# Adapters with transposes three units behind, y's two parts taken straight from PSUM, and a shared normalisation

## Chip, cores and metric

One core of one Trainium2 chip. The metric is the device time of one execution in microseconds. The kernel before: median 1236.32 us of three runs (1235.46, 1236.32, 1237.9).

## The reference

`x` is (4, 512, 512) in float32: 4 sequences of 512 positions, 512 features. Layer 0 is attention, two GELU networks with a hidden size of 2048 and a clip to 0..1 (its result is called y0 here). The change leaves it alone. Then come three adapters, L1 to L3, of the same form, with weights picked by sequence out of three experts:

```python
h = jnp.einsum('bsh,bhk->bsk', hidden_states, W_down[role]) + b_down[role][:, None, :]
h = jax.nn.gelu(h, approximate=False)          # (4, 512, 256)
u = jnp.einsum('bsk,bkh->bsh', h, W_up[role]) + b_up[role][:, None, :]
y = hidden_states + u
mean = jnp.mean(y, axis=-1, keepdims=True)
var = jnp.mean(jnp.square(y - mean), axis=-1, keepdims=True)
yn = (y - mean) * jax.lax.rsqrt(var + LN_EPS)
return yn * gamma[role][:, None, :] + beta[role][:, None, :]
```

## The kernel before

The kernel is written with hand-made queues: a fixed order of instructions for each engine, semaphores between them. Layer 0 fills the first 1057 us. The adapters follow as twelve **units**: unit u is layer u // 4 of sequence u % 4. So unit u needs the result of unit u - 4. All products are made in three passes of fp32r: an operand is kept as a high part and a low part, and `mm3` (L538) multiplies high by high, high by low, low by high.

A unit goes through these stages:

- down products D(u), `t_down_mm` (L692): 24 matmuls 128x512 from yT[u % 4] (features on partitions, high and low part) into two PSUM banks (`down_bank`)
- `h_gelu` (L1019) on ACT: GELU with the down bias into hf, then a cast to the high part in h_hl; `h_lo` (L1405) on DVE: the low part
- up products U(u), `t_up_mm` (L713): 24 matmuls into banks 0 to 3 (`UP`), positions on partitions
- `z_stats` (L1416) on DVE: four tiles, each the sum of PSUM and the residual rows `res` into z, then bn_stats and bn_aggr
- GpSimd (POOL, L1509): ve and rstd of a unit, two small instructions; `factors` (L1399) on DVE: nmr = -mean x rstd
- `z_norm` (L1013) on ACT: z = z x rstd + nmr, four tiles in place
- POOL (L1525, L1527): the residual rows of unit u + 4, res = z x gamma + (beta + next up bias), eight instructions of 128x512 a unit (units 0 to 7)
- transposes T(u), `t_transpose` (L727): 16 transposes of z into four PSUM banks (`tr_bank`, L198)
- `y_scale` (L1033) on ACT: yf = T x gamma + beta for four tiles out of PSUM, then four casts to yT's high part; `y_lo` (L1450) on DVE: low part = yf - high part. For units 8 to 11 the scaled tiles are the output instead

The order of the work is that of four loops over steps s. PE (L753): D(s), U(s-1), T(s-2). ACT (L1048): z_norm(s-2), h_gelu(s), y_scale(s-2). DVE (L1465): h_lo(s), z_stats(s-1) with the factors of s-1 at its end, y_lo(s-2). POOL: for each unit rstd, then all its residual rows. In steps 0 to 2, y0 of sequences 1 to 3 is transposed to rows on PE (`y0_to_rows`, L674) and the first up bias added by DVE (`y0_rows`, L1389). z has two buffers, at u % 2. For the last two units (`FINE`, L339) rstd and factors are made in halves; the last unit's z tiles 1 and 3 are normalised by DVE (`norm_tile`, L1410) and its output tiles 1 and 3 scaled by DVE (`out_scale`).

SP issues all loads and stores in order. `unit_columns` (L480) loads gamma, beta and down bias of a unit as columns into one of four places (`pp`), from unit 4 on after y_scale(u-4). Around it stand the loads of weights (`unit_down`, `unit_up`) and of the rows for POOL (`unit_rows`). Line L509 loads y0 of sequence 1.

Of the kernel before, what the change touches and what calls it, by code (L numbers as in the profile page):

```python
# [12 lines left out]
P = 128  # L13
B = 4
# [84 lines left out]
def build(nc, wts, xin, bias_in, codes_in, experts_in, up_w, dn_w, wdu_all, pp_all, gb_all,  # L99
          bup_all, out):  # L100
    ctx = ExitStack()
    with ctx:
# [48 lines left out]
        z = [at("z0", 104, [P, DT, V]), at("z1", 136, [P, DT, V])]  # L151
# [19 lines left out]
        pp = sm[:, 84:124].rearrange("p (b n) -> p b n", b=B)  # L171
# [99 lines left out]
        t_pp = [sem(f"unit_columns_landed_{i}") for i in range(B)]  # L271
# [67 lines left out]
        FINE = 10  # L339
# [23 lines left out]
        def _(sp):  # L363
# [116 lines left out]
            def unit_columns(u, layer, b):  # L480
                if u >= B:
                    sp.wait_ge(t_yf, (u - 4) * DT + DT)
                row = layer * EXPERTS + ex[b]
                sp.dma_start(pp[:, b, :], pp_all[bass.ds(row, 1)].rearrange("o p n -> (o p) n")).then_inc(t_pp[b], 16)
# [18 lines left out]
            for b in range(B):  # L503
                sp.dma_start(bup0[:, b, :], bup_all[bass.ds(ex[b], 1)].to_broadcast([P, V])).then_inc(t_bup0, 16)
                unit_columns(b, 0, b)
            sp.wait_ge(aop_used, PAIRS * AOP)
            unit_up(0)
# [7 lines left out]
            for u in range(2, 14):  # L515
                if u < 12:
                    unit_down(u)
                    if u >= B:
                        unit_columns(u, u // B, u % B)
# [17 lines left out]
        def _(pe):  # L537
# [154 lines left out]
            def t_down_mm(u, b):  # L692
                pe.wait_ge(t_wd[u % 2], 16 * (u // 2 + 1))
                for m in range(MT):
# [3 lines left out]
                    elif u == 2:  # L698
                        pe.wait_ge(t_hf, (u - 2) * MT + m + 1)
                    else:  # L700
                        pe.wait_ge(t_yf, (u - 3) * DT + m + 1)
# [25 lines left out]
            def t_transpose(u, b):  # L727
                for d in range(DT):
                    if u == 11:
                        pe.wait_ge(t_z, 12 * DT)  # L730
                    elif u == 10 and d >= 2:
                        pe.wait_ge(t_yf, (u - 1) * DT + d - 1)
                    elif d >= 2:
                        pe.wait_ge(t_hf, (u + 2) * MT + d - 1)
                    elif u:
                        pe.wait_ge(t_yf, (u - 1) * DT + d + 3)
                    else:
                        pe.wait_ge(t_hf, MT + d + 1)
                    for i in range(DT):
                        if d == 0 and u == 11:  # L740

                            if i % 2:
                                pe.wait_ge(t_znv, i // 2 + 1)
                            else:
                                pe.wait_ge(t_zn, 11 * DT + i // 2 + 1)
                        elif d == 0:
                            pe.wait_ge(t_zn, u * DT + (i + 1))
                        ins = nc.tensor.transpose(tr_bank(u, d)[:, i * P:(i + 1) * P],
                                                  z[b % 2][:, i, d * P:(d + 1) * P], ident[:, :])
# [3 lines left out]
            for s in range(14):  # L753
                if s < 12:
                    t_down_mm(s, s % B)
                if s == 0:
                    y0_to_rows(1)
                if 1 <= s < 13:
# [3 lines left out]
                if 2 <= s:  # L762
                    t_transpose(s - 2, (s - 2) % B)
# [3 lines left out]
        def _(act):  # L767
# [245 lines left out]
            def z_norm(u, tiles=range(DT)):  # L1013
                for i in tiles:
                    act.wait_ge(t_nmr, nmr_count(u, i))
                    nc.scalar.activation(z[u % 2][:, i, :], z[u % 2][:, i, :], ACT.Identity,  # L1016
                                         scale=rstd[:, u % 2, i:i + 1], bias=nmr[:, u % 2, i:i + 1]).then_inc(t_zn, 1)

            def h_gelu(u):  # L1019
                for m in range(MT):  # L1020
                    act.wait_ge(t_down, u * MT + m + 1)
                    if m == 0:
                        act.wait_ge(t_pp[u % B], 16 * (u // B + 1))
                    if u > 0:
                        act.wait_ge(t_hlo, (u - 1) * MT + m + 1)
                    nc.scalar.activation(hf[m][:, :], down_bank(u, m), ACT.Gelu, bias=pp[:, u % B, 8 + m:9 + m]).then_inc(t_hf, 1)
# [5 lines left out]

            def y_scale(u, tiles=range(DT)):  # L1033

                for d in tiles:
                    act.wait_ge(t_tr, u * DT + d + 1)
                    if 1 <= u < 8:
                        act.wait_ge(t_ylo, (u - 1) * DT + d + 1)
                    dst = yf[d][:, :] if u < 8 else res[:, u % B, d, :]
                    nc.scalar.activation(dst, tr_bank(u, d), ACT.Identity,  # L1040
                                         scale=pp[:, u % B, d:d + 1], bias=pp[:, u % B, 4 + d:5 + d]).then_inc(t_yf, 1)
                if u < 8:
                    for d in range(DT):
                        act.wait_ge(t_yf, u * DT + d + 1)
                        nc.scalar.copy(yT[u % B][:, 0, d, :], yf[d][:, :]).then_inc(t_yhi, 1)
# [20 lines left out]
        def _(dve):  # L1066
# [343 lines left out]
            def norm_tile(i):  # L1410

                dve.wait_ge(t_nmr, nmr_count(11, i))
                nc.vector.tensor_scalar(z[1][:, i, :], z[1][:, i, :], rstd[:, 1, i:i + 1], nmr[:, 1, i:i + 1],
                                        ALU.mult, ALU.add).then_inc(t_znv, 1)

            def z_stats(u):  # L1416

                for i in range(DT + 2):
                    if i < DT:
# [3 lines left out]
                        if u >= 2:  # L1423

                            if u < 10:
                                dve.wait_ge(t_rmul, (u - 2) * DT + i + 1)
                            dve.wait_ge(t_tr, (u - 1) * DT)
# [156 lines left out]
```

## Time and profile before

| | |
|---|---|
| median of three runs | 1236.32 us |
| the profiled execution | 1239.01 us |
| its span, first to last instruction | 1236.9 us |
| PE (matmuls) busy | 1191.9 us, 96% |
| DVE busy | 807.4 us, 65% |
| ACT busy | 567.0 us, 46% |
| POOL busy | 173.5 us, 14% |
| granted TensorE clock, mean | 0.994 |
| adapters | about 1057 us to the end |

The page's second part shows the span in 40 equal slices of 31 us. Each digit is the busy share in tenths, 9 is 90% or more. The adapters are the last six slices:

```profile
PE   7999999799999899999999999989999999999997
DVE  5444385746766766565766666686665565879986
POOL 1332230000000000000000000000000000488871
PEclk9999999899999999999999999999999999999999
```

PE is TensorE's matmuls, DVE VectorE, ACT ScalarE, POOL GpSimd, SP the engine that issues the loads (its queue is SPq). L12 is line 12 of the kernel. A "releaser" is the instruction whose semaphore ended an idle time. Records of neighbouring instructions on ACT and DVE overlap by some 0.1 us, so the step from one start to the next is shorter than a record.

### The profile page before, as it was taken

The page shows a single profiled execution, that of the slowest core. Times are in us where ns is not written, and L with a number is a line of the kernel's source. Part 1 is how long each engine was busy: PE and PEld are TensorE (multiplying, and loading weights), DVE is VectorE, ACT ScalarE, POOL GpSimd, SP SyncE. Part 2 cuts the span into 40 slices and gives each one's busy share as a digit, 9 for nine tenths or more (in the row PEclk, how much of TensorE's full clock was granted, in tenths as well). Part 3 has the DMA queues.
Part 4 walks back from the last instruction along what each step waited for, and adds up shares of the span by engine and source line. Part 5 has one row for each costly group of instructions (what it writes and reads, how often), then busy time and mean ns, then how long its engine had stood idle before and what let it go on. Part 6 is the DMA issues. An engine that isn't in the chain of part 4 may idle for free.

```text
span 1236.9 us, 15228 instructions
## 1 busy us (share of the span) xinstructions
PE 1191.9 (96%) x5312; PEld 973.7 (79%) x5312; DVE 807.4 (65%) x1461; ACT 567.0 (46%) x1068; POOL 173.5 (14%) x147
## 2 busy tenths in 40 slices
PE   7999999799999899999999999989999999999997
PEld 5878878677788688888887787768888888788776
DVE  5444385746766766565766666686665565879986
ACT  5334353554533534343524633544343433266666
POOL 1332230000000000000000000000000000488871
PEclk9999999899999999999999999999999999999999
DMA  5755452114312202020461221411111118655534
GB/s 189 271 199 180 162 176 85 43 43 153 122 58 77 87 16 94 10 94 9 169 274 51 88 83 51 171 51 51 52 52 52 52 34 322 229 189 193 175 137 170
DMA packets 51186, 145.82 MB, mean 118 GB/s; under 512 B 6420, under 2 KB 6420, under 8 KB 46886
## 3 DMA queue, kind: packets, MB, share of 16 engines
q1 hardware_dynamic: 51110, 144.84, 33.2%
q8 instruction: 43, 0.70, 0.2%
q14 instruction: 33, 0.27, 0.1%
HBM read 108.11 MB, written 36.71 MB: 117 GB/s over the span
## 4 chain that ended last, share of the span: by engine, by line
PE 71%; DVE 11%; POOL 8%; ACT 4%; issue 4%; DMA 1%; SPq 0%; POOLq 0%; DVEq 0%; ACTq 0%
PE psum L541 70%; POOL res L1525 3%; POOL res L1527 3%; DVE ring L1187 1%; DMA prep<-wdu_dram 1%; ACT z L1016 1%; ACT ring L877 1%; POOL sm L1518 1%; DVE g_hl L1254 1%; DVE sm L1434 1%; DVE res L1269 1%; DVE res L1324 1%; DVE w_t L1228 0%; DMA wk_raw<-wts_dram 0%; POOL prep L1498 0%
## 5 line engine op out<-in xcount | busy, mean ns | idle before, releaser
L541 PE MATMUL psum<-g_hl,w_hl 128*128 128x512 f32 x1536 | 353.3, 390 | 1.5 <-DVE g L1242 1.3
L541 PE MATMUL psum<-a_op,ring 128*128 128x512 f32 x1344 | 324.4, 394 | 17.5 <-DVE w_t L1228 11.1
L541 PEld LDWEIGHTS psum<-g_hl,w_hl 128*128 128x128 f32 x1536 | 287.9, 188 | 64.6 <-DVE g L1242 4.8
L541 PEld LDWEIGHTS psum<-a_op,ring 128*128 128x128 f32 x1344 | 252.9, 190 | 77.8 <-DVE w_t L1228 14.5
L541 PE MATMUL psum<-c_op,ring 128*128 128x512 f32 x672 | 166.1, 394 | 0.6 <-DVE c_op L1296 0.6
L1254 DVE TENSOR_TENSOR g_hl<-g,g_hl 128x512 fp32r<-128x512 f32 x128 | 87.7, 691 | 111.7 <-ACT g_hl L917 110.4
L541 PEld LDWEIGHTS psum<-c_op,ring 128*128 128x128 f32 x672 | 127.3, 190 | 28.5 <-DVE c_op L1296 2.0
L1506 POOL TENSOR_TENSOR yT<-res,yT 128x512 fp32r<-128x512 f32 x8 | 11.7, 1487 | 875.6 <-ACT yT L1011 875.6
L877 ACT CAST ring<-asum 128x256 fp32r<-128x256 f32 x192 | 76.2, 403 | 122.3 <-PE psum L541 100.9
L917 ACT CAST g_hl<-g 128x512 fp32r<-128x512 f32 x128 | 78.3, 618 | 101.1 <-PE psum L541 101.1
L1187 DVE TENSOR_TENSOR ring<-asum,ring 128x256 fp32r<-128x256 f32 x192 | 80.8, 422 | 63.8 <-ACT ring L877 61.3
L894 ACT ACTIVATE g<-g,sm 128x512 f32<-128x512 f32 x96 | 69.6, 725 | 109.9 <-DVE g L1234 47.5
L1187 DVE TENSOR_TENSOR ring<-rawp,ring 128x256 fp32r<-128x256 f32 x144 | 60.8, 422 | 81.0 <-ACT ring L877 81.0
L1269 DVE TENSOR_TENSOR res<-psum,res 128x512 f32<-128x512 f32 x96 | 64.8, 691 | 24.1 <-PE psum L541 24.0
L877 ACT CAST ring<-rawp 128x256 fp32r<-128x256 f32 x144 | 57.0, 403 | 46.3 <-PE psum L541 46.2
L541 PE MATMUL psum<-yT,wd 128*128 128x512 f32 x288 | 68.6, 394 | 6.0 <-issue 6.0
L1498 POOL TENSOR_TENSOR prep<-prep 128x512 f32<-128x512 f32 x36 | 51.6, 1437 | 131.4 <-ACT prep L788 131.4
L541 PE MATMUL psum<-wu,h_hl 128*128 128x512 f32 x288 | 67.4, 390 | 0.0
L541 PEld LDWEIGHTS psum<-yT,wd 128*128 128x128 f32 x288 | 53.1, 188 | 18.0 <-issue 7.3
L541 PEld LDWEIGHTS psum<-wu,h_hl 128*128 128x128 f32 x288 | 54.0, 188 | 11.2
L1016 ACT ACTIVATE z<-z,sm 128x512 f32<-128x512 f32 x46 | 33.9, 808 | 37.7 <-DVE sm L1402 37.7
L1525 POOL TENSOR_TENSOR res<-z,bc 128x512 f32<-128x512 f32 x32 | 48.2, 1507 | 12.4 <-ACT z L1016 12.4
(124 smaller groups left out, 1381.2 us busy)
## 6 DMA issues: line engine op xcount, KB each, us to landing
rawp<-up_w_dram SPq DMA_DIRECT2D x48, 512.0 KB, 3.6
wdu_split<-prep SPq DMA_DIRECT2D x36, 512.0 KB, 2.9
wraw<-dn_w_dram SPq DMA_DIRECT2D x64, 256.0 KB, 3.1
wd<-wdu_split SPq DMA_DIRECT2D x12, 1024.0 KB, 7.3
wu<-wdu_split SPq DMA_DIRECT2D x12, 1024.0 KB, 5.4
prep<-wdu_dram SPq DMA_DIRECT2D x36, 256.0 KB, 3.3
second_pair_operands<-c_op SPq DMA_DIRECT2D x7, 1024.0 KB, 6.9
a_op<-second_pair_operands SPq DMA_DIRECT2D x7, 1024.0 KB, 11.3
```

What stands on the lines that cost most here:

```text
L541: ins = nc.tensor.matmul(ps, lw(el), rw(er), start=first and i == 0, stop=last and i == 2, skip_group_check=skip)
L877: nc.scalar.copy(ring[n % RING][:, 0, :], aop_src(n)).then_inc(aop_hi, 1)
L894: nc.scalar.activation(dst, src, ACT.Gelu, bias=(cb1, mb1)[l][:, t:t + 1]).then_inc(gelu_done, 1)
L917: nc.scalar.copy(g_hl[t % GHL][:, 0, :], g[:, q, 2 * row + seq, :]).then_inc(g_hi_done, 1)
L1016: nc.scalar.activation(z[u % 2][:, i, :], z[u % 2][:, i, :], ACT.Identity, scale=rstd[:, u % 2, i:i + 1], bias=nmr[:, u % 2, i:i + 1]).the ...
L1187: nc.vector.tensor_tensor(ring[n % RING][:, 1, :], aop_src(n), f(ring[n % RING][:, 0, :]), ALU.subtract).then_inc(aop_lo, 1)
L1254: nc.vector.tensor_tensor(g_hl[t % GHL][:, 1, :], g[:, q, 2 * row + seq, :], f(g_hl[t % GHL][:, 0, :]), ALU.subtract).then_inc(g_lo_done, 1)
L1269: nc.vector.tensor_tensor(dst, bank[4 * seq + m], dst, ALU.add).then_inc(d_evac, 1)
L1324: nc.vector.tensor_scalar(res[:, 2 + seq, m, :], res[:, 2 + seq, m, :], 0.0, 1.0, ALU.max, ALU.min).then_inc(y0_done, 1)
L1498: nc.gpsimd.tensor_tensor(prep[i][:, 1, :], prep[i][:, 1, :], prep[i][:, 0, :], ALU.subtract).then_inc(p_lo, 1)
L1525: nc.gpsimd.tensor_tensor(res[:, u % B, i, :], z[i2][:, i, :], bc[i2][:, 0, :], ALU.mult).then_inc(t_rmul, 1)
L1527: nc.gpsimd.tensor_tensor(res[:, u % B, i, :], res[:, u % B, i, :], bc[i2][:, 1, :], ALU.add).then_inc(t_res, 1)
```

## The change

Seven things are changed, all in the adapters.

1. PE transposes a unit one step later: D(s), T(s-3), U(s-1). The banks of the transposes change: tiles 0 and 1 go to UP[2] and UP[3], tiles 2 and 3 to the down banks of the same parity. The up products of tiles 2 and 3 wait until tiles 0 and 1 of y (unit u - 2) have been read out by DVE.
2. z has three buffers (u % 3).
3. `y_split` and `y_less_high` take the place of y_scale's first part, the casts and y_lo for units 0 to 7. ACT makes yT's high part straight from PSUM (T x gamma + beta, rounded). DVE makes yf = T x gamma - high part from PSUM with one scalar_tensor_tensor a tile, and ACT adds beta to it, which is the low part.
4. Every unit's z tiles 0 and 2 are normalised by ACT, 1 and 3 by DVE (`norm_tile`), ahead of y_less_high in DVE's order.
5. ACT's step: GELU(s), y_split(s-3), h_hi(s), z_norm(s-2). DVE's step: factors(s-2), two norm_tiles, y_less_high(s-3), z_stats(s-1), h_lo(s).
6. POOL's order for a unit: rstd(u), residual rows 2 and 3 of u - 1, residual rows 0 and 1 of u.
7. All twelve units' columns are loaded at once, at a place of their own, after the last use of layer 0's operands. Only the last unit is made in halves (`FINE` 11).

```diff
-        z = [at("z0", 104, [P, DT, V]), at("z1", 136, [P, DT, V])]
+        z = [at(f"z{i}", k, [P, DT, V]) for i, k in enumerate((104, 136, 128))]
...
-            return bank[4 + 2 * ((u % 2) ^ (1 if d < 2 else 0)) + d % 2]
+            if u == 10:
+                return bank[4 + d]
+            return UP[2 + d] if d < 2 else bank[4 + 2 * (u % 2) + d - 2]
...
+            for u in range(LAYERS * B):
+                unit_columns(u)
...
+                    if u >= 2 and i >= 2:
+                        pe.wait_ge(t_yf, (u - 2) * DT + i - 1)
...
-            for s in range(14):
+            for s in range(15):
                 if s < 12:
                     t_down_mm(s, s % B)
                 if s == 0:
                     y0_to_rows(1)
+                if 3 <= s:
+                    t_transpose(s - 3, (s - 3) % B)
                 if 1 <= s < 13:
                     t_up_mm(s - 1, (s - 1) % B)
                 if 1 <= s < 3:
                     y0_to_rows(s + 1)
-                if 2 <= s:
-                    t_transpose(s - 2, (s - 2) % B)
...
-            def z_norm(u, tiles=range(DT)):
-                for i in tiles:
+            def z_norm(u):
+                for i in (0, 2):
                     act.wait_ge(t_nmr, nmr_count(u, i))
-                    nc.scalar.activation(z[u % 2][:, i, :], z[u % 2][:, i, :], ACT.Identity,
+                    nc.scalar.activation(z[u % 3][:, i, :], z[u % 3][:, i, :], ACT.Identity,
                                          scale=rstd[:, u % 2, i:i + 1], bias=nmr[:, u % 2, i:i + 1]).then_inc(t_zn, 1)
...
+            def y_split(u):
+
+                for d in range(DT):
+                    act.wait_ge(t_tr, u * DT + d + 1)
+                    nc.scalar.activation(yT[u % B][:, 0, d, :], tr_bank(u, d), ACT.Identity,
+                                         scale=pp[:, u, d:d + 1], bias=pp[:, u, 4 + d:5 + d]).then_inc(t_yhi, 1)
+                for d in range(DT):
+                    act.wait_ge(t_yf, u * DT + d + 1)
+                    nc.scalar.activation(yT[u % B][:, 1, d, :], yf[d][:, :], ACT.Identity,
+                                         bias=pp[:, u, 4 + d:5 + d]).then_inc(t_ylo, 1)
...
-            for s in range(12):
-                if 2 <= s < 11:
-                    z_norm(s - 2)
-                h_gelu(s)
-                if s == 11:
-                    z_norm(9)
+            for s in range(14):
+                if s < 12:
+                    h_gelu(s)
+                if 3 <= s < 11:
+                    y_split(s - 3)
+                if 11 <= s:
+                    y_scale(s - 3)
+                if s < 12:
+                    h_hi(s)
                 if s == 0:
                     y0_hi(3)
                 if 2 <= s:
-                    y_scale(s - 2)
-            z_norm(10)
-            y_scale(10)
-            z_norm(11, (0, 2))
+                    z_norm(s - 2)
             y_scale(11, LAST_BY[0])
...
+            def norm_tile(u, i):
+
+                dve.wait_ge(t_nmr, nmr_count(u, i))
+                nc.vector.tensor_scalar(z[u % 3][:, i, :], z[u % 3][:, i, :], rstd[:, u % 2, i:i + 1], nmr[:, u % 2, i:i + 1],
                                         ALU.mult, ALU.add).then_inc(t_znv, 1)
...
+            def y_less_high(u):
                 for d in range(DT):
                     dve.wait_ge(t_yhi, u * DT + d + 1)
-                    nc.vector.tensor_tensor(yT[u % B][:, 1, d, :], yf[d][:, :], f(yT[u % B][:, 0, d, :]), ALU.subtract).then_inc(t_ylo, 1)
+                    if u >= 1:
+                        dve.wait_ge(t_ylo, (u - 1) * DT + d + 1)
+                    nc.vector.scalar_tensor_tensor(out=yf[d][:, :], in0=tr_bank(u, d), scalar=pp[:, u, d:d + 1], in1=f(yT[u % B][:, 0, d, :]),
+                                                   op0=ALU.mult, op1=ALU.subtract).then_inc(t_yf, 1)
...
             for s in range(13):
-                if s < 12:
-                    h_lo(s)
+                if 2 <= s:
+                    factors(s - 2, 0, DT)
+                    norm_tile(s - 2, 1)
+                    norm_tile(s - 2, 3)
+                if 3 <= s < 11:
+                    y_less_high(s - 3)
                 if s == 0:
                     y0_rows(1)
                 if 1 <= s < 13:
                     z_stats(s - 1)
                 if 1 <= s < 3:
                     y0_rows(s + 1)
-                if 2 <= s < 10:
-                    y_lo(s - 2)
-            norm_tile(3)
+                if s < 12:
+                    h_lo(s)
             out_scale(11)
...
+            def next_rows(u, tiles):
+
+                pool.wait_ge(t_bc[u % 2], 32 * (u // 2 + 1))
+                for i in tiles:
+                    pool.wait_ge((t_zn, t_znv)[i % 2], 2 * u + i // 2 + 1)
+                    nc.gpsimd.tensor_tensor(res[:, u % B, i, :], z[u % 3][:, i, :], bc[u % 2][:, 0, :], ALU.mult).then_inc(t_rmul, 1)
                     pool.wait_ge(t_rmul, u * DT + i + 1)
-                    nc.gpsimd.tensor_tensor(res[:, u % B, i, :], res[:, u % B, i, :], bc[i2][:, 1, :], ALU.add).then_inc(t_res, 1)
+                    nc.gpsimd.tensor_tensor(res[:, u % B, i, :], res[:, u % B, i, :], bc[u % 2][:, 1, :], ALU.add).then_inc(t_res, 1)
+
+            for u in range(12):
+                rstd_of(u)
+                if 1 <= u < 9:
+                    next_rows(u - 1, (2, 3))
+                if u < 8:
+                    next_rows(u, (0, 1))
```

The rest of the diff renames the buffers and their semaphore counts to fit: rstd of u waits for z_norm and norm_tile of u - 2 each, z's writing waits for T(u-3) and for POOL's reading of u - 3, and D(u) for u >= 4 waits until y_less_high(u-4) has read the down banks.

## Rows read from the trace of the kernel before

**Rows 1.** Window view, one unit: us, busy PE, PEld, DVE, ACT, POOL, clock, DMA share, GB/s

```profile
1142.80:1157.50 14.70, 13.24 (x66) 10.66 (x65) 13.18 (x20) 9.86 (x17) 13.02 (x10) 1.00 0.52 179
```

**Rows 2.** Chain of waits, one unit: start us, us, what

```profile
1142.78 0.82 ACT z L1016
1143.74 1.37 POOL res L1525
...
1154.58 1.29 POOL res L1527
1156.22 1.03 POOL sm L1518
1157.47 0.82 ACT z L1016
```

**Rows 3.** Timeline of PE where nothing holds it: start us, us, instructions

```profile
1067.06 5.72 PE L541 MATMUL psum<-yT,wd 128*128 128x512 f32 x24
1072.62 5.61 PE L541 MATMUL psum<-wu,h_hl 128*128 128x512 f32 x24
1078.06 1.91 PE L688 MATMUL psum<-ident,res 128*128 128x128 f32 x16
...
1079.72 5.70 PE L541 MATMUL psum<-yT,wd 128*128 128x512 f32 x24
...
1090.71 1.69 PE L688 MATMUL psum<-ident,res 128*128 128x128 f32 x12
```

**Rows 4.** Timeline of the other engines in one unit, same columns

```profile
1142.66 4.67 DVE L1453 TENSOR_TENSOR yT<-yf,yT 128x512 fp32r<-128x512 f32 x4
...
1146.76 1.13 ACT L1031 CAST h_hl<-hf 128x512 fp32r<-128x512 f32 x2
...
1147.40 3.31 DVE L1408 TENSOR_TENSOR h_hl<-hf,h_hl 128x512 fp32r<-128x512 f32 x2
...
1150.63 1.27 DVE L1428 TENSOR_TENSOR z<-psum,res 128x512 f32<-128x512 f32 x2
...
1155.54 0.29 DVE L1440 BATCH_NORM_AGGREGATE sm<-sm 128x2 f32<-128x6 f32 x2
```

**Rows 5.** Source view of one DVE line, and its timeline beside GpSimd's subtractions

```profile
L1324 DVE TENSOR_SCALAR res<-res x8: 417/962/1529, 1057.0 to 1062.7; 128x512 f32<-128x512 f32 x8
...
1059.83 1.51 DVE L1324 TENSOR_SCALAR res<-res 128x512 f32<-128x512 f32 x1
1061.27 1.51 DVE L1324 TENSOR_SCALAR res<-res 128x512 f32<-128x512 f32 x1
```

**Rows 6.** Source views of lines: duration ns min/median/max

```profile
L1413 DVE TENSOR_SCALAR z<-z,sm x2: 545/546/546, 1228.5 to 1230.1; 128x512 f32<-128x512 f32 x2
...
L1428 DVE TENSOR_TENSOR z<-psum,res x48: 650/674/692, 1075.3 to 1225.9; 128x512 f32<-128x512 f32 x48
...
L1266 DVE SCALAR_TENSOR_TENSOR res<-psum,sm,res x16: 750/751/751, 455.9 to 876.9; 128x512 f32<-128x512 f32 x16
...
L894 ACT ACTIVATE g<-g,sm x96: 722/725/728, 228.5 to 1035.4; 128x512 f32<-128x512 f32 x96
```

**Rows 7.** Timeline of VectorE at factors(1) and factors(8)

```profile
1095.84 0.16 DVE L1402 SCALAR_TENSOR_TENSOR sm<-sm 128x4 f32<-128x4 f32 x1 [1.42 <-POOL sm L1518]
...
1201.37 0.16 DVE L1402 SCALAR_TENSOR_TENSOR sm<-sm 128x4 f32<-128x4 f32 x1 [1.45 <-POOL sm L1518]
```

**Rows 8.** Timelines of the tail: VectorE, then PE

```profile
1218.72 0.66 DVE L1428 TENSOR_TENSOR z<-psum,res 128x512 f32<-128x512 f32 x1
...
1220.56 0.16 DVE L1440 BATCH_NORM_AGGREGATE sm<-sm 128x2 f32<-128x6 f32 x1
...
1220.12 5.71 PE L541 MATMUL psum<-wu,h_hl 128*128 128x512 f32 x24
```

**Rows 9.** Timeline of the load queue, and the landing of one load

```profile
1048.74 0.34 SPq L509 DMA_DIRECT2D res<-y_spill  x1
...
DMA to landing us min/median/max: 10.8/10.8/10.8
```

More of the change, by code:

```diff
@@ L270, in build @@
         t_wu = [sem(f"up_weights_landed_{i}") for i in range(2)]
-        t_pp = [sem(f"unit_columns_landed_{i}") for i in range(B)]
+        t_pp = sem("unit_columns_landed")
         t_bc = [sem(f"unit_rows_landed_{i}") for i in range(2)]
@@ L337, in y_ready @@
             return (t_yf, u * DT + by_act.index(d) + 1) if d in by_act else (t_yv, by_dve.index(d) + 1)
-        FINE = 10
+        FINE = 11
         LAST_BY = (0, 2), (1, 3)
@@ L478, in unit_up, with unit_columns @@
                              split_sets[bass.ds(u // B * EXPERTS + ex[b], 1), DT * KB // PC:NPC].rearrange("o c p e n -> p e (o c) n")).then_inc(t_wu[u % 2], 16)
[L480 to L484, printed above, removed]
+            def unit_columns(u):
+                row = u // B * EXPERTS + ex[u % B]
+                sp.dma_start(pp[:, u, :], pp_all[bass.ds(row, 1)].rearrange("o p n -> (o p) n")).then_inc(t_pp, 16)
             def unit_rows(u, layer, b):
@@ L730, in t_transpose @@
                         pe.wait_ge(t_z, 12 * DT)
-                    elif u == 10 and d >= 2:
-                        pe.wait_ge(t_yf, (u - 1) * DT + d - 1)
+                    elif u == 10:
+                        pe.wait_ge(t_yf, (u - 2 + d // 2) * DT + d % 2 + 3)
                     elif d >= 2:
@@ L1021, in h_gelu, with h_hi @@
                     act.wait_ge(t_down, u * MT + m + 1)
-                    if m == 0:
-                        act.wait_ge(t_pp[u % B], 16 * (u // B + 1))
+                    if u == 0 and m == 0:
+                        act.wait_ge(t_pp, 16 * LAYERS * B)
                     if u > 0:
                         act.wait_ge(t_hlo, (u - 1) * MT + m + 1)
-                    nc.scalar.activation(hf[m][:, :], down_bank(u, m), ACT.Gelu, bias=pp[:, u % B, 8 + m:9 + m]).then_inc(t_hf, 1)
+                    nc.scalar.activation(hf[m][:, :], down_bank(u, m), ACT.Gelu, bias=pp[:, u, 8 + m:9 + m]).then_inc(t_hf, 1)
+            def h_hi(u):
                 for m in range(MT):
@@ L1036, in y_scale @@
                     act.wait_ge(t_tr, u * DT + d + 1)
[L1037 to L1045, printed above, removed]
-            y0_hi(2)
-            for s in range(12):
-                if 2 <= s < 11:
-                    z_norm(s - 2)
-                h_gelu(s)
-                if s == 11:
-                    z_norm(9)
+                    nc.scalar.activation(res[:, u % B, d, :], tr_bank(u, d), ACT.Identity,
+                                         scale=pp[:, u, d:d + 1], bias=pp[:, u, 4 + d:5 + d]).then_inc(t_yf, 1)
+            y0_hi(2)
+            for s in range(14):
[7 more added lines that the diff above has]
+                    h_hi(s)
                 if s == 0:
@@ L1422, in z_stats @@
                             dve.wait_ge(t_res, (u - B) * DT + i + 1)
[L1423 to L1427, printed above, removed]
-                        nc.vector.tensor_tensor(z[u % 2][:, i, :], UP[i], res[:, u % B, i, :], ALU.add).then_inc(t_z, 1)
+                        if u >= 3:
+                            if u < 11:
+                                dve.wait_ge(t_rmul, (u - 3) * DT + i + 1)
+                            dve.wait_ge(t_tr, (u - 2) * DT)
+                        nc.vector.tensor_tensor(z[u % 3][:, i, :], UP[i], res[:, u % B, i, :], ALU.add).then_inc(t_z, 1)
                     if 1 <= i < DT + 1:
@@ L1442, in z_stats @@
                         factors(u, 0, 2)
-                if u == 11:
-                    norm_tile(1)
                 if u >= FINE:
+                    norm_tile(u, 1)
                     factors(u, 2, 2)
-                else:
-                    factors(u, 0, DT)
-            def y_lo(u):
+                    norm_tile(u, 3)
+            def y_less_high(u):
                 for d in range(DT):
                     dve.wait_ge(t_yhi, u * DT + d + 1)
-                    nc.vector.tensor_tensor(yT[u % B][:, 1, d, :], yf[d][:, :], f(yT[u % B][:, 0, d, :]), ALU.subtract).then_inc(t_ylo, 1)
+                    if u >= 1:
+                        dve.wait_ge(t_ylo, (u - 1) * DT + d + 1)
+                    nc.vector.scalar_tensor_tensor(out=yf[d][:, :], in0=tr_bank(u, d), scalar=pp[:, u, d:d + 1], in1=f(yT[u % B][:, 0, d, :]),
+                                                   op0=ALU.mult, op1=ALU.subtract).then_inc(t_yf, 1)
             def out_scale(u):
@@ L1458, in out_scale @@
                     dve.wait_ge(t_tr, u * DT + d + 1)
-                    nc.vector.tensor_scalar(res[:, u % B, d, :], tr_bank(u, d), pp[:, u % B, d:d + 1], pp[:, u % B, 4 + d:5 + d],
+                    nc.vector.tensor_scalar(res[:, u % B, d, :], tr_bank(u, d), pp[:, u, d:d + 1], pp[:, u, 4 + d:5 + d],
                                             ALU.mult, ALU.add).then_inc(t_yv, 1)
@@ L1508, in _, with rstd_of @@
             pool.wait_ge(s_half, 1)
-            for u in range(12):
+            def rstd_of(u):
                 i2 = u % 2
```

38 lines of the change are left out of this document (11 added, 27 removed).

## Prediction

> **What bounds the kernel now.** Read the table of 40 slices on the page first: PE is busy at 9 tenths in nearly every slice at a granted clock of 0.9 or more, so the first 1057 us are TensorE's matter and the change leaves them as they are. What is left is the adapters, the last 180 us. There the table of windows [rows 1] shows something else: a unit takes 14.70 us, PE is busy 13.24 us of it, DVE 13.18 and POOL 13.02, so no busy share decides. The chain of waits does [rows 2]: it never goes through PE, but round a loop of ACT, POOL and DVE. ACT normalises tile 0 of a unit (1142.78), POOL starts the next layer's residual rows 0.96 us later, works eight row operations until 1155.87 and then the two small ones for rstd until 1157.25; DVE makes the shifts, ACT normalises the next unit at 1157.47. One turn is 14.69 us, and the turns from the third unit to the ninth are alike. POOL idles in it only while it waits for ACT. PE without a hold [rows 3] needs 5.55 us for the down products (1067.06 to 1072.62), 5.44 for the up products (to 1078.06) and 1.66 for sixteen transposes (to 1079.72): 12.65 us. So 2.0 us a unit are to be won by a better order and no more, about 15 us over seven units.
>
> In what follows F(u) is the moment at which DVE starts factors(u), the shifts of unit u. In the trace F(1) is 1095.84 and F(8) is 1201.37 [rows 7]; from F(8) to the end of the span are 35.5 us.
>
> **The change, part by part.** The third z buffer and POOL's new order (rstd of u, rows 2 and 3 of u-1, rows 0 and 1 of u) are meant to let POOL work through. They take the wait for ACT off rows 2 and 3, but rows 0 and 1 of u still stand ahead of rstd of u+1, and they wait for tile 0 of unit u, which ACT normalises at the very end of its step. I follow that loop, since every instruction of it is in program order:
>
> F(u), DVE: factors, 0.16 us [rows 7] and 0.04 until the next starts: 0.20.
>
> DVE: norm_tile(u,1) and norm_tile(u,3). Alone such an instruction takes 0.55 us (L1413) [rows 6]. But POOL starts rows 2 and 3 of u-1 as soon as rstd is made, about 0.1 us ahead of the first norm_tile. What a scale-and-shift from SBUF to SBUF costs DVE beside a POOL tensor_tensor is in [rows 5]: 417 ns alone, but 1.51 us each, one every 1.44 us, while POOL subtracts: each waits out one whole POOL operation. The first norm_tile then ends 1.55 us after its issue and the second 1.44 later: 3.0. Bounds: 1.1 (both free, 2 x 0.55), 2.0 (one free, one held), 3.0 (both held). I take 3.0, as four such instructions in a row were held (two of them stand in the rows).
>
> By the Trainium skill, "SBUF — State Buffer", section "Who interferes with whom", a tensor_scalar can run in a mode that takes the port pair shared with GpSimd, and whoever starts second is blocked for the whole instruction. The 1.51 us of [rows 5] agree. By that rule alone, whoever issues first decides, so it would give 1.1 if DVE came first; that is the rival below.
>
> DVE: y_less_high(u-1, 0), a scalar_tensor_tensor with one input in PSUM: 0.75 (L1266) [rows 6]. Held or not? The z addition has the same kinds of places, PSUM and SBUF in, SBUF out, and was at most 0.69 us in 48 (L1428) [rows 6] although POOL was busy beside most of them. I take it as free; its upper bound is that of the old y_lo, which has both inputs in SBUF: 4.67 us for four [rows 4].
>
> ACT: hand-over 0.05, then y_split's second half. Its four activations follow DVE's 0.67 us steps (0.75 less the overlap of records): three steps, 2.0, and the last with 0.05 and 0.57 until the next starts, since a bias-only activation from SBUF has a record of 0.725 (L894) [rows 6]: 2.62. Bounds 2.6 and 2.9 (the 0.82 of z_norm, which also scales).
>
> ACT: h_hi, two casts in 1.02 (the record of 1.13 [rows 4] less the overlap). ACT: z_norm(u,0) and hand-over to POOL: 0.96 [rows 2].
>
> POOL: rows 0 and 1, four operations. Eight took 12.13 us [rows 2], 1.52 each with DVE's contending operations beside them; DVE's h_lo will again lie in this stretch (3.31 us for two where POOL is active, [rows 4]). Four at 1.52: 6.08; bounds 5.2 (four of 1.29 alone) and 6.9 (four at up to 1.72).
>
> POOL: rstd of u+1, 1155.87 to 1157.25: 1.38, and 0.03 to DVE. Then F(u+1).
>
> Sum: 0.20 + 3.0 + 0.75 + 0.05 + 2.62 + 1.02 + 0.96 + 6.08 + 1.38 + 0.03 = 16.1 us a unit, against 14.69. In general it is 13.1 + N, with N the time of the two norm_tiles.
>
> Does anything else close later? DVE's own step is 0.2 + 3.0 + 2.75 + 5.2 for z_stats (1150.63 to 1155.83, [rows 4]) + 3.3 for h_lo = 14.5: it idles 1.6 us for the factors. POOL's is 12.1 + 1.4 = 13.5. PE: the up products now wait at tile 2 for y_less_high of the transposes in the same banks, that is F + 3.95; half of the up products, down products, transposes and the other half are 12.65 us, so PE idles some 3.4 us a unit, ahead of tile 2 above all. The y parts come in time for the down products (first at F + 4.7, wanted at F + 6.7). Making the y parts directly from PSUM removes 2.19 us of copies from ACT's hi path and DVE's 4.67 us become 2.75; both lie on engines that then wait, apart from what the sum above holds.
>
> **Ahead of the loop.** D(3) no longer has T(0) before it, and U(1) ends at 1090.7 as before [rows 3]. DVE then has the last addition and statistics (2.0, as 1218.72 to 1220.72 in [rows 8], from 1090.9), the fourth residual (four at 0.62, as the z addition's record of 0.69 less overlap) and now h_lo(2) ahead of factors(1), beside POOL's rows: 2 x 1.6. F(1) is 1090.9 + 2.0 + 2.5 + 3.2 = 1098.6, 2.8 later than before. Column loads: twelve instead of four are issued before the weights and y0 of sequence 1. Eight more at some 0.5 us of queue are 4 us; y0 of sequence 1 was issued at 1048.74 and landed in 10.8 [rows 9], at 1059.5, and PE transposes it directly ahead of D(1), which starts at 1067.06 [rows 3]; the sixteen transposes take 1.7 us and end there, so some 5 us hide it. I put it at nothing; 0 to 2 us if the queue is slowed twice as much. The later loads lose their column load and the wait ahead of it, which were no bound.
>
> **The tail.** From F(8): up products of unit 9 go on at F + 3.95 and end at 6.7, D(11) at 12.25, T(8) at 13.9, U(10) at 19.35; DVE ends the statistics of unit 10 at 21.4 (0.2 and 2.0 behind), and only then h_lo(11), 0.6 each: U(11) can begin at 22.1. Before, it began at 1220.12 and the span ended 16.8 us after that [rows 8]; what follows U(11) is unchanged. So 38.9 us instead of 35.5: +3.4 (36 + N in general).
>
> **The sum.** 1098.6 + 7 x 16.1 + 38.9 = 1250.2 us of span, against 1236.9: +2.8 ahead of the loop, +7.2 in seven turns (112.7 against 105.5), +3.4 in the tail, 13.4 in all. The profiled execution took 1239.01 us, 2.1 more than its span and 2.7 more than the median of the runs; I add the difference to the median: 1236.32 + 13.4 = 1249.7.
>
> **The rivals.** (1) The norm_tiles find the port free (N = 1.1). DVE's chain from rstd to the first norm_tile is 0.23 us and POOL's next start some 0.1, so it is a race that the profile of before does not show. If DVE wins it and keeps the port for both, F(1) is 1097, the turn 14.2, the tail 37.1: 1233.5 of span, 1232.9 us. This is the case on the other side; in terms of N the span is 1223.8 + 8.8 N, so it decides below N = 1.5. (2) One held, one free: N = 2.0, 1241.4 of span, 1240.8 us. (3) The loop does not bind, because ACT's tile is early by something I overlook, and PE's 12.65 us do: 1097 + 88.6 + 37.1 = 1222.7, 1222.1 us. For it: the busy sums of ACT and DVE fall. Against it: each step of the loop is held by program order or by a semaphore. (4) y_less_high is held by POOL too, two of four, some 1.1 more each: eight turns (tail included) of 2.2 more, 1267 us. Against it: the record of L1428 [rows 6].
>
> **Chances.** Forecast, 1245 to 1254: 0.47. Rival 2, up to 1244: 0.16. Rival 4: 0.04. Rival 1: 0.14, a mixture of 1 and 2 within 0.2% of before: 0.09. Rival 3: 0.10. A difference of 0.2% (2.5 us) is about what a measurement of this kernel tells from none. So faster 0.24, same 0.09, slower 0.67. The range of eight in ten leaves out rival 3 and rival 4: 1231 to 1255, where the lower bound of POOL's rows (0.9 a turn) is only reached together with rival 1's N.
>
> **What would show it.** A turn of the chain near 16 us that goes through DVE norm, y_less_high, ACT y_split, h_hi, z_norm, POOL rows and rstd; norm_tile records of 1.5 to 1.6 us for units 1 to 8 and 0.55 for 9 to 11; y_less_high at 0.75; PE idle before L541, released by DVE's y_less_high, about 3 us a unit; DVE waiting for POOL's rstd. Wrong would be: norm_tiles at 0.55 throughout, a chain that stays on PE, POOL without idle time, or an h_lo that is late for the up products.

## The result: slower by 1.6%, the loop was right, one of its terms was not

Median of four runs 1258.94 us (1254.94 to 1260.75) against 1237.11 us for the kernel before (four runs, one more than the 1236.32 us above rest on). The ratio is 1.0164, 95% interval 1.0142 to 1.0186. I had forecast 1249.7 with 1231 to 1255: the right sign, 13.4 us where 21.8 were measured, and the time lies above the range. The profiled execution took 1258.94 us, its span 1257.2 (before 1236.9).

The busy sums are no guide: in the changed kernel ACT is busy 8.7 us less (558.3 us) and POOL 4.2 us less (169.3), and DVE 16.4 us more (823.8). The windows view of one unit of the changed kernel, columns as in [rows 1]:

```profile
1146.55:1163.62 17.07, 14.60 (x66) 11.84 (x65) 14.48 (x22) 9.25 (x15) 12.43 (x11) 0.90 0.45 156
```

A unit takes 17.07 us (before 14.70), no engine is full, and the granted clock is 0.90 instead of 1.00. The chain of waits over the same unit, start us, us, what, in place of the chain in [rows 2]:

```profile
1146.55 1.27 DVE sm L1401
1148.60 0.64 issue
1149.37 1.48 DVE z L1412
1150.85 0.67 DVE yf L1451
1151.54 2.00 ACT yT L1038 x3
1153.62 0.53 issue
1154.15 1.12 ACT h_hl L1028 x2
1155.27 0.73 ACT z L1011
1156.13 1.31 POOL res L1527
1157.51 1.30 POOL res L1529
1158.81 1.70 POOL res L1527
1160.59 1.61 POOL res L1529
1162.29 0.19 POOL sm L1518
1162.57 1.03 POOL sm L1520
1163.62 1.26 DVE sm L1401
```

L1401 are the factors, L1412 norm_tile, L1451 y_less_high, L1038 the second half of y_split, L1028 h_hi, L1011 z_norm, L1527 and L1529 residual rows, L1520 rstd. It is the loop that the prediction summed, link by link. One turn is 17.07 us here and 17.04 on the mean of the six from the second on. The first link is the surprise: 1.27 us for an instruction on four numbers a partition, 0.16 in [rows 7]. Who stands beside it is in the timelines of DVE and POOL:

```profile
1146.55 1.26 DVE L1401 SCALAR_TENSOR_TENSOR sm<-sm 128x4 f32<-128x4 f32 x1 [2.56 <-POOL sm L1520]
1147.84 3.00 DVE L1412 TENSOR_SCALAR z<-z,sm 128x512 f32<-128x512 f32 x2
1150.77 2.71 DVE L1451 SCALAR_TENSOR_TENSOR yf<-psum,unit_columns,yT 128x512 f32<-128x512 f32 x4
...
1146.49 1.30 POOL L1527 TENSOR_TENSOR res<-z,bc 128x512 f32<-128x512 f32 x1
1147.87 1.29 POOL L1529 TENSOR_TENSOR res<-res,bc 128x512 f32<-128x512 f32 x1
1149.12 1.44 POOL L1527 TENSOR_TENSOR res<-z,bc 128x512 f32<-128x512 f32 x1
```

POOL's row begins at 1146.49, DVE's factors at 1146.55, and they end together, at 1147.8. Then each norm_tile waits out one more POOL operation and ends 0.3 us behind it. By the records the first norm_tile starts 0.03 us before that operation (1147.84 against 1147.87) and is still the one that waits, so starts this close do not show who came first. y_less_high is not held: four in 2.71 us, the first two of them beside a POOL operation (1150.64 to 1151.97). PE in the same unit:

```profile
1146.18 3.01 PE L540 MATMUL psum<-wu,h_hl 128*128 128x512 f32 x12
1151.65 4.57 PE L540 MATMUL psum<-wu,h_hl 128*128 128x512 f32 x12 [2.47 <-DVE yf L1451]
1156.06 5.64 PE L540 MATMUL psum<-yT,wd 128*128 128x512 f32 x24
```

It does tiles 0 and 1 of the up products, idles 2.47 us for y_less_high (forecast 3.4), and then takes 4.4 us for tiles 2 and 3 instead of 2.7. The windows view tells why; the clock is the column behind POOL's:

```profile
1149.20:1151.65 2.45, 0.00 (x0) 0.03 (x1) 2.45 (x4) 0.11 (x1) 2.37 (x2) 1.00 0.00 0
1151.65:1156.06 4.41, 4.41 (x12) 3.50 (x13) 4.41 (x8) 4.41 (x8) 0.32 (x1) 0.61 0.37 123
1156.06:1161.54 5.48, 5.48 (x25) 4.46 (x24) 5.00 (x10) 1.32 (x2) 5.25 (x4) 1.00 0.67 219
```

After the idle stretch the granted clock is 0.61 on the mean, mostly the 1.2 GHz level, and 1.00 again for the down products. The prediction had no term for this. It gives a second account of the same 17.07 us: PE's own 12.65, 2.5 of waiting and 1.7 of low clock also make 16.9. The experiments had to tell the two apart.

### The profile page after: what moved, and what is told of

Its sections match the earlier page's. It is cut to its first block, busy times and chain, and to the rows that moved or that the text cites. A ratio compares the mean times of both kernels' runs of the same rounds, so it can differ in the third digit from the quotient of the medians.

```text
span 1257.2 us, 15252 instructions
## 1 busy us (share of the span) xinstructions
PE 1201.5 (96%) x5312; PEld 981.5 (78%) x5312; DVE 823.8 (66%) x1482; ACT 558.3 (44%) x1046; POOL 169.3 (13%) x145
## 4 chain that ended last, share of the span: by engine, by line
PE 71%; DVE 12%; ACT 5%; POOL 5%; issue 4%; DMA 2%; SPq 0%; DVEq 0%; POOLq 0%; ACTq 0%
PE psum L540 70%; DMA prep<-wdu_dram 2%; POOL res L1527 2%; POOL res L1529 2%; DVE ring L1186 1%; ACT yT L1038 1%; DVE z L1412 1%; ACT ring L872 1%; DVE sm L1401 1%; DVE g_hl L1253 1%; POOL sm L1520 1%; ACT h_hl L1028 1%; POOL prep L1500 1%; DVE res L1323 1%; DVE res L1268 1%
## 5 line engine op out<-in xcount | busy, mean ns | idle before, releaser
L540 PEld LDWEIGHTS psum<-a_op,ring 128*128 128x128 f32 x1344 | 252.7, 189 | 77.7 <-DVE w_t L1227 14.6
L540 PE MATMUL psum<-wu,h_hl 128*128 128x512 f32 x288 | 81.3, 442 | 19.6 <-DVE yf L1451 19.0
L540 PEld LDWEIGHTS psum<-wu,h_hl 128*128 128x128 f32 x288 | 60.1, 213 | 35.6 <-issue 22.5
L1527 POOL TENSOR_TENSOR res<-z,bc 128x512 f32<-128x512 f32 x32 | 46.0, 1438 | 37.1 <-ACT z L1011 37.1
L896 ACT COPY u_t<-psum 128x512 f32<-128x512 f32 x32 | 18.8, 587 | 61.6 <-PE psum L540 61.6
```

Source lines behind the costliest of these rows:

```text
L540: ins = nc.tensor.matmul(ps, lw(el), rw(er), start=first and i == 0, stop=last and i == 2, skip_group_check=skip)
L896: nc.scalar.copy(u_t[:, :], bank[4 * q + BANK_OF[P1]]).then_inc(u_done, 1)
L1527: nc.gpsimd.tensor_tensor(res[:, u % B, i, :], z[u % 3][:, i, :], bc[u % 2][:, 0, :], ALU.mult).then_inc(t_rmul, 1)
```

## The experiments

Ratios are to the kernel before on the same chip. Turns are read from one factors instruction to the next in DVE's timeline. In some of the diffs only the lines that matter are shown; waits and semaphore counts follow them.

**GpSimd kept off the port until DVE is done.** Work unchanged, one wait more:

```diff
                 rstd_of(u)
                 if 1 <= u < 9:
+                    pool.wait_ge(t_znv, 2 * u + 2)
                     next_rows(u - 1, (2, 3))
```

> The changed kernel with one wait more: GpSimd waits, after rstd of u, for both of DVE's norm_tiles before it starts the residual rows of u - 1. The work is the same. Two theories. Loop: the unit of 17.05 us is the closed chain factors, two norm_tiles, y_less_high, ACT's second half of y_split, h_hi, z_norm, four residual-row operations, rstd; three DVE instructions in it are each held by one GpSimd operation (factors 1.26 instead of 0.16, two norm_tiles 2.95 instead of 1.0). With GpSimd kept off the port until they are done the turn falls by 3.05 to 14.0, over seven turns and the tail by some 24 us, to about 1234 us. Clock: the unit is TensorE's own, 12.65 us of work, 2.5 of waiting for y_less_high and 1.7 us because the granted clock is 0.61 for the half of the up products after that wait. A wait added on GpSimd then gives at most what the clock costs, 1.7 a unit, 1245 us, or nothing (1259), as GpSimd is busier for it.

Measured: 1234.27 us, ratio 0.9974 (0.9961 to 0.9986). A wait on GpSimd took 24.7 us off the changed kernel. From DVE's timeline:

```profile
1151.13 0.16 DVE L1401 SCALAR_TENSOR_TENSOR sm<-sm 128x4 f32<-128x4 f32 x1 [2.56 <-POOL sm L1520]
1151.33 1.00 DVE L1412 TENSOR_SCALAR z<-z,sm 128x512 f32<-128x512 f32 x2
```

The factors are back at 0.16 us, two norm_tiles take 1.00 together, and the turn is 14.0 us (1137.12 to 1151.13). What ends last now is GpSimd itself: 1.3 us of the new wait, eight rows, rstd.

**The normalisation back on ACT.** z_norm makes all four tiles of units 0 to 10, the two norm_tiles are gone from DVE's step:

```diff
-                for i in (0, 2):
+                for i in (0, 2) if u == 11 else range(DT):
...
-                    norm_tile(s - 2, 1)
-                    norm_tile(s - 2, 3)
```

> The changed kernel with the shared normalisation undone: ACT normalises all four tiles of units 0 to 10 at the same place of its step, DVE none. Loop theory: the two norm_tiles leave the loop, 2.95 us a turn (factors are still held by GpSimd), the extra tiles of ACT come behind tile 0 and beside GpSimd's rows: turn 14.1 us, about 1234 us. Clock theory: the wait of TensorE becomes shorter and the clock is kept, at most 1.7 us a unit, 1245 us.

Measured: 1235.4 us, ratio 0.9983 (0.9973 to 0.9992), turn 14.0 us (1138.34 to 1152.33), the factors still at 1.25 us. So taking the shared normalisation out of the changed kernel gives back 23.5 us. The chain of waits is still the loop of the prediction, without its norm_tiles.

**TensorE kept busy.**

```diff
+                    if 2 <= u < 10 and i == 2:
+                        pe.wait_ge(t_hf, (u + 1) * MT + 1)
+                        for _ in range(9):
+                            nc.tensor.matmul(down_bank(u + 1, 0), h_hl[b % 2][:, 0, 0, 0:P], wu[b % 2][:, 0, 0, :],
+                                             start=True, stop=True)
```

> The changed kernel with TensorE kept busy: for units 2 to 9, nine matmuls into the unused down bank stand between tiles 1 and 2 of the up products, in the time in which TensorE otherwise waits for y_less_high; their result is never read. Loop theory: the granted clock stays at 1.0 and tiles 2 and 3 take 2.7 us instead of 4.4, but the turn stays at 17.05 us, since TensorE is not in the loop; only the tail gains the 1.7 us: 1257 us. Clock theory: 1.7 us a unit over eight units are won: 1245 us.

Measured: 1258.09 us, ratio 1.0163 (1.0144 to 1.0181). PE's timeline shows the nine matmuls (L722) ahead of tiles 2 and 3 in two units that follow each other:

```profile
1134.58 4.62 PE L540 MATMUL psum<-wu,h_hl 128*128 128x512 f32 x12 [2.03 <-DVE yf L1456]
...
1149.02 2.20 PE L722 MATMUL psum<-wu,h_hl 128*128 128x512 f32 x9
1151.63 3.03 PE L540 MATMUL psum<-wu,h_hl 128*128 128x512 f32 x12 [0.42 <-DVE yf L1456]
```

Behind the fillers 0.42 us of waiting are left in every second unit, and there the half takes 3.03 us at a granted clock of 1.00. In the units between, 2.03 us are left and it takes 4.62 us at 0.62. The mean clock of the execution is 0.991 instead of 0.983. Yet all turns from the second on are alike, 17.02 to 17.07 us, with the fast half and with the slow one, and as without the fillers. The clock account falls: here PE has slack enough to hide it, except in the tail.

**Other orders that cut the loop.** First, on GpSimd, four rows of the unit before, for which nothing is late:

```diff
-                    next_rows(u - 1, (2, 3))
-                if u < 8:
-                    next_rows(u, (0, 1))
+                    next_rows(u - 1, range(DT))
```

> The changed kernel with another order on GpSimd: rstd of u, then all four residual rows of u - 1, so that it never waits for a tile that ACT normalises late in the same step. Loop theory: the loop is cut between z_norm and GpSimd. What is left is DVE's own step with its instructions held by GpSimd: 1.3 for factors, 2.95 norm_tiles, 2.65 y_less_high, 5.3 statistics, 2.5 to 3.3 h_lo, together 14.7 to 15.5 us: a turn of 15.1, about 1244 us. Clock theory: 1245 us at best, 1259 if TensorE still waits over 2 us a unit.

Measured: 1237.1 us, ratio 0.9999 (0.9986 to 1.0011), turn 14.15 us. I had summed DVE's step to 15.1: h_lo was not held (1.26 us for two), because GpSimd has finished its rows by then. The factors and norm_tiles are held as before (1.24 and 3.03). The new loop is statistics, rstd, factors, norm_tiles, y_less_high, statistics.

Second, on ACT, z_norm ahead of what waits for DVE:

```diff
-                    y_split(s - 3)
+                    y_split(s - 3, 0)
+                    z_norm(s - 2)
+                    y_split(s - 3, 1)
```

> The changed kernel with z_norm(s-2) moved up in ACT's step, between the first and the second half of y_split(s-3). Everything else, the held DVE instructions too, stays. Loop theory: GpSimd gets its tile 2 us after the factors and no longer waits; what is left is DVE's step with its held instructions: 1.3 + 2.95 + 2.65 + 5.3 + 2.5 = 14.7 us, against 13.3 for GpSimd; about 1241 us. Rival (the held instructions alone make the loss, where z_norm stands makes none): 1259 us.

Measured: 1237.54 us, ratio 1.0004 (0.9992 to 1.0017), turn 14.15 us. Either cut ends in the same DVE loop. The holds still count in it, but less: the kernel below that has this order on GpSimd and no norm_tiles has a turn of 12.67 us.

**The factors' own share.**

```diff
+                    pool.wait_ge(t_nmr, u + 1)
                     next_rows(u - 1, (2, 3))
```

> The changed kernel with one wait on GpSimd, for the factors of u alone, ahead of the residual rows of u - 1. The factors then cost 0.16 us instead of 1.26, as my prediction had priced them, and the norm_tiles meet GpSimd as before. If both are still held (the prediction's price) the turn is 17.05 - 1.1 = 15.95 us and the time 1250 us, near the predicted 1249.7. If the first norm_tile comes ahead of GpSimd, whose wait ends at the same moment, the two take about 2.0 instead of 2.95: a turn of 15.0, 1242 us. If the length of the factors were of no weight: 1259 us.

Measured: 1248.75 us, ratio 1.0101 (1.0079 to 1.0123), turn 15.99 us (1142.79 to 1158.78). From the timelines of DVE and POOL:

```profile
1142.79 0.16 DVE L1401 SCALAR_TENSOR_TENSOR sm<-sm 128x4 f32<-128x4 f32 x1 [2.56 <-POOL sm L1520]
1142.98 3.04 DVE L1412 TENSOR_SCALAR z<-z,sm 128x512 f32<-128x512 f32 x2
...
1143.03 1.29 POOL L1527 TENSOR_TENSOR res<-z,bc 128x512 f32<-128x512 f32 x1 [0.28 <-DVE sm L1401]
```

The mean turn is 15.97 us, 1.07 less than in the changed kernel, and close to the forecast 16.1. Both norm_tiles are held, although the record of the first starts 0.05 us before POOL's. That the whole time is the predicted one within 1 us is partly luck: the span of 1246.8 us is 3.4 below the forecast, with F(1) 4.4 us earlier and the tail 1.3 us longer.

**The split of y alone, in the kernel before.** ACT makes the high part from PSUM, DVE T x gamma less the high part, ACT adds beta; otherwise only the wait ahead of the column loads changes. DVE's part of the edit:

```diff
-                    nc.vector.tensor_tensor(yT[u % B][:, 1, d, :], yf[d][:, :], f(yT[u % B][:, 0, d, :]), ALU.subtract).then_inc(t_ylo, 1)
+                    nc.vector.scalar_tensor_tensor(out=yf[d][:, :], in0=tr_bank(u, d), scalar=pp[:, u % B, d:d + 1], in1=f(yT[u % B][:, 0, d, :]),
+                                                   op0=ALU.mult, op1=ALU.subtract).then_inc(t_yf, 1)
```

> The kernel before with one part of the change alone: y's high part by ACT straight from PSUM, T x gamma less the high part by DVE from PSUM, beta added by ACT. Its own order of work, two z buffers, normalisation by ACT. Loop theory: the loop of before was factors, z_norm, eight residual-row operations, rstd, 14.69 us. Now ACT's second half of y_split stands between factors and z_norm: it waits for DVE's y_less_high, which DVE makes after the factors. That adds 0.75 + 0.05 + 2.6 us and takes off some 0.6, as y_lo no longer holds GpSimd: a turn of 17.4 us, about 1257 us. Rival: the part only takes 2.2 us of casts from ACT and 2 us from DVE, which nothing waits for, and frees GpSimd's port: a turn of 14.1, 1232 us.

Measured: 1277.23 us, ratio 1.0337 (1.0311 to 1.0362), the slowest of all, and 20 us above the theory. PE's timeline shows what I had not counted; below it a line of DVE's:

```profile
1145.65 1.91 PE L748 MATMUL psum<-ident,z 128*128 128x128 f32 x16
1151.88 8.56 PE L541 MATMUL psum<-yT,wd 128*128 128x512 f32 x24 [4.32 <-issue]
...
1151.03 2.73 DVE L1454 SCALAR_TENSOR_TENSOR yf<-psum,sm,yT 128x512 f32<-128x512 f32 x4
```

The down products write into the banks of the transposes, which DVE now frees only after the statistics, rstd and factors of the next unit. The profile names no releaser for the wait, but PE starts at 1151.88, 0.1 us after the first of the four y_less_high (L1454) ends. So PE is in the loop, and waits 4.3 us in it. And the 24 matmuls behind that wait take 8.4 us here, at a granted clock of 0.64, and 6.9 to 8.1 in the other units of the loop, instead of 5.6. The turns from unit 2 to unit 8 are 18.5 to 19.7 us. To see the clock's share, 18 matmuls into a free bank fill the wait of units 4 to 10:

```diff
+                if 4 <= u < 11:
+                    pe.wait_ge(t_z, (u - 2) * DT + 1)
+                    for _ in range(18):
+                        nc.tensor.matmul(UP[0], wd[b % 2][:, 0, 0, 0:P], yT[(u - 1) % B][:, 0, 0, :], start=True, stop=True)
```

> The kernel before with the split of y alone (b_split_only, 1277 us), and 18 matmuls into the free bank UP[0] ahead of the down products of units 4 to 10, where TensorE waited 4.3 us and then worked 8.4 us instead of 5.6 at a low clock. Their result is never read. Theory: in that kernel TensorE is in the loop itself (up products, statistics, rstd, factors, y_less_high, down products), so the 2.8 us of low clock count in full: a turn of 16.5 to 17.4 instead of 19.0, 1260 us. Rival: the clock is not what lengthens it, or GpSimd's own loop of 17.4 and more holds: 1270 to 1277 us.

Measured: 1262.62 us, ratio 1.0218 (1.019 to 1.0245), turns of 17.13 us:

```profile
1143.87 4.34 PE L697 MATMUL psum<-yT,wd 128*128 128x512 f32 x18
1148.32 5.74 PE L541 MATMUL psum<-yT,wd 128*128 128x512 f32 x24
```

The down products are back at 5.6 us and a granted clock of 1.00. The kernel is 14.6 us faster for 126 matmuls more. Here the low clock does count, since PE is in the loop.

**A version ahead of both.** GpSimd's rows of u - 1 and the normalisation on ACT together, the edits as above:

> The changed kernel with both: GpSimd's four residual rows of u - 1 after rstd of u, and all four tiles normalised by ACT. With rows_after alone the turn was 14.15 us: factors held 1.24, norm_tiles 2.95, y_less_high 2.64, statistics 5.2, rstd and its hand-overs 2.1. Without the norm_tiles that loop is 11.2 us; TensorE's own work is 12.65 us and GpSimd's 8 x 1.4 and 1.4 for rstd is 12.6 to 12.9. Loop theory: a turn of 12.9 us, 7 x 1.1 less than the 14.0 of norm_act alone: about 1228 us. If the gains of the two are one and the same: 1235 us.

Measured: 1228.57 us, ratio 0.9939 (0.9917 to 0.9962). Most turns are 12.65 to 12.7 us, PE's own work, where I had expected GpSimd to hold at 12.9. Two turns are 14.3 and 14.2 us; PE's waits in the run say why:

```profile
PE psum L546 <- DMA wd<-wdu_split: 2.5, 2, 1.3
```

With the faster turn the down weights come late: their load stands in SP's queue behind the row loads, which wait for GpSimd. Moved:

```diff
-                if 4 <= u < 10:
-                    unit_rows(u - 2, (u - 2) // B, (u - 2) % B)
+                if 5 <= u < 11:
+                    unit_rows(u - 3, (u - 3) // B, (u - 3) % B)
```

> As b_rows_after_norm_act (1228.6 us), with the load of a unit's residual-row factors one step later in SP's queue, behind the next unit's down weights. In that run TensorE waited 1.35 and 1.18 us for down weights, as the queue stood behind GpSimd's rows, and two turns were 14.2 us instead of 12.7. Those two waits go, and every turn is 12.7: 2.5 us less, 1226 us. If another wait takes their place at once: 1228.6.

Measured: 1227.91 us, ratio 0.992 (0.9894 to 0.9946). The waits for weights are gone and the turns all 12.65 to 12.7, but the medians are 0.7 us apart, inside the noise. The traces do show the gain: from D(0), the first down products, to the end of the span are 169.3 us instead of 171.7. But D(0) itself began 2.6 us later in this execution, for a reason that no trace shows, and the last 14 transposes ran at a granted clock of 0.50, and took 3.25 us instead of 1.75. In step 11, h(11)'s parts first, on ACT and in the same way on DVE:

```diff
+                if s == 11:
+                    h_hi(s)
                 if 3 <= s < 11:
                     y_split(s - 3)
                 if 11 <= s:
                     y_scale(s - 3)
-                if s < 12:
+                if s < 11:
                     h_hi(s)
```

> As rows_after_norm_act, and in step 11 ACT makes the high part of h(11) ahead of y_scale(8), DVE its low part ahead of the statistics of unit 10. In the changed kernel h_lo(11) came 2 us after the last sum of unit 10 and TensorE waited 0.6 us for it, and 0.35 us for a sum. Both should go: 1.0 us less than without, about 1227 us.

Measured: 1227.67 us, ratio 0.993 (0.9906 to 0.9955); 0.9 us better than without, which the intervals don't separate. In the trace the 0.61 us of waiting for h_lo(11) are gone; the 0.35 us for a sum, which I had expected to go too, are still there. With both:

> As c_loads_first, with h(11)'s two parts ahead of y_scale(8) and of the statistics of unit 10: TensorE's 0.6 us of waiting for h_lo(11) go. 1225.3 us, unless the last transposes run at the low clock, which costs 1.4 us.

Measured: 1224.95 us, ratio 0.9899 (0.9876 to 0.9923): 12 us faster than the kernel before and 34 us faster than the changed one. It keeps the change's later transposes, third z buffer, split of y and single load of columns, and drops the interleaved rows and, but for the last unit, the shared normalisation. How much each of the parts that are kept brings by itself, no run tells.

## Why the prediction was right in its sign and short in its size

- **What bounds, and the loop.** Right. Each link stood in the chain of the changed kernel in the order given, and four ways to cut or shorten it gave back 21 to 25 us.
- **factors: the step that failed.** Priced at 0.16 us from a row in which GpSimd was idle. It is a scalar_tensor_tensor with both inputs in SBUF, issued 0.06 us after GpSimd's row, and waits it out: 1.26 us, +1.1 a turn. I had applied the rule to norm_tile and, without a reason, not to the instruction ahead of it. c_factors_wait shows the term: the turn falls by 1.07 us. The whole 10.2 us between the two kernels (1258.94 to 1248.75) are more than this term: the same wait also freed h_lo(2), 1.20 us ahead of factors(1) instead of 2.72, and the second half of U(9) ran at full clock there, 1.6 us shorter.
- **norm_tiles.** Right: 3.0 forecast, 2.93 from 1147.84 to 1150.77. As factors end together with one POOL operation, the norm_tiles wait out the next two. Only in the first turn were they 1.97 us.
- **y_less_high, y_split, h_hi, z_norm, rows, rstd.** Right: 0.77 us from 1150.77 to 1151.54 (forecast 0.80), then 2.61, 1.02, 0.96, 6.08 and 1.38, all within 0.01 us.
- **Ahead of the loop.** F(1) came at 1096.44, 2.2 us before the forecast. PE began D(0) 1.7 us earlier in this execution (1056.21 against 1057.90). The change doesn't explain it: over all the executions D(0) began between 1052.7 and 1057.9, behind the same layer 0. And h_lo(2) took 2.7 us instead of 3.2. The column loads cost nothing, as said. The first turn was 16.07 us and the other six 17.04.
- **The tail.** 42.5 us against 38.9. Of the 3.6, factors are 1.1 and the low clock of U(9)'s second half 1.7 (with the filler matmuls the tail is 40.5 us). U(11) began 3.1 us behind the end of U(10) instead of 2.75, and from its start to the end were 17.2 us instead of 16.8. There the last fourteen transposes took 2.75 us at a granted clock of 0.61, against 1.75 in the kernel before; of that 1.0 only 0.4 reached the end.
- **The sum.** Span 1257.2 against 1250.2: -2.2 ahead of the loop, +5.6 in the turns (118.3 against 112.7), +3.6 in the tail: 7.0 us. The other 2.2 us of the 9.2 come from the step to the median. I had taken the profiled execution as 2.7 us above it, as in the kernel before; here it was the median itself.
- **The range** ended at 1255, and the only case above it was one more hold, on y_less_high, with a chance of 0.04. The right case, a hold on factors, was missing from the list, and so was the low clock.
- **Rivals.** Rival 1's race is lost in all turns, but its price fits a_port_wait, where the port is kept free: a turn of 14.0 (14.2 said) and 1234.27 us (1232.9 said). That is partly luck, since another chain, GpSimd's own with the new wait, ends last there. Rival 2, one norm_tile held, is seen in the first turn alone. Rival 3 is false for the changed kernel; its turns of 12.7 us come in b_rows_after_norm_act, after the loop is cut. Rival 4 is false: no y_less_high was held.

By the Trainium skill, "SBUF — State Buffer", section "Who interferes with whom", a VectorE instruction with two SBUF inputs contends with a GpSimd instruction that reads SBUF, and the second to start is blocked until the first ends. The factors at 1.26 us beside 0.16 show that this holds for four elements a partition too; it stood on the page, and I had not used it for this instruction. Who starts second, the records decide for the factors (0.06 us behind POOL) and not for the norm_tiles, whose records start 0.03 to 0.05 us before the POOL operation that they wait out.

## What to carry to other kernels

Before an instruction is moved between two engines, write out the closed chain in program order through all engines and price each link with what runs beside it, the smallest links too: what a held instruction cost here was the holder's length, not its own (1.26 us beside an operation of 1.30, 0.16 alone). An engine that has slack should start its long operations after the short ones that others wait for: one added wait on GpSimd was worth 25 us in this kernel. A hand-over from ACT to DVE and back takes work off both, and puts both into one chain: with the old order it cost 40 us. The kernels that carry it without such a loss have the later transposes and the third z buffer too; which of the two makes the room, no run separates.

## What the runs showed of the hardware

- A DVE instruction on 128x4 with both inputs in SBUF took 1.26 us instead of 0.16 beside a GpSimd tensor_tensor that had begun 0.06 us earlier. A scalar_tensor_tensor with one input in PSUM took 734 to 741 ns in all 32 cases, GpSimd active or not.
- In the changed kernel TensorE idle for 2.5 us was followed by 4.4 us at a granted clock of 0.61, in every unit. It is no rule: in c_factors_wait idle times of 3.0 us were followed by 4.2 to 4.3 us at 0.64 in two units, and by 2.8 us at 1.00 in two others. The low clock costs time only where PE is in the loop: nothing measurable in a_filler, 14.6 us between b_split_only and c_split_filler. The last transposes of near-identical kernels, after the same 2.36 us of idle time, came at 1.75 us in one execution and 3.25 in another. What decides between them stays open.
- An order of work that closes a loop a little differently can be compared by its turn: 17.04, 15.97, 14.15, 14.00 and 12.67 us gave 1258.9, 1248.8, 1237.1, 1234.3 and 1224.9 to 1228.6 us.
- The same layer 0 did not always take the same time: in fourteen profiled executions the adapters' first down products began between 1052.68 and 1057.90 us. So spans of single executions that are under 5 us apart are better compared from that point on.
